# Low parts of the second gates ahead of phi's square sums in halves, and the first loop's rounding ahead of its normalising

## The chip, the cores and the metric

One core of a Trainium2 chip. The metric is the device time of the whole kernel in microseconds (us), here the median of 3 runs. Engines: PE (TensorE), DVE (VectorE), ACT (ScalarE), POOL (GpSimd), SP (queue of DMA issues).

## The reference, cut to what matters

One layer of a small language-model tower on 2 x 1024 tokens, width 192 (D), in float32:

```python
def _L0_tok_ref(input_ids, link_ids, wte, gamma, beta, W_proj, W_val, W_out, value_traces):
    tok = wte[input_ids]
    Q = _layer_norm(tok, gamma, beta) @ W_proj.T        # 8 heads of 64
    V = tok @ W_val.T
    Q_store, V_store = Q[:, :, :-2, :], V[:, :, 2:, :]  # Q_store masked by the link ids
    Q_erase = Q_store / norm(Q_store)
    erase = einsum('bhip,bhiq->hpq', Q_erase, einsum('bhip,hpq->bhiq', Q_erase, value_traces)) / denom
    traces = 0.99 * (value_traces - erase) + 0.1 * einsum('bhip,bhiq->hpq', Q_store, V_store) / denom
    return (shifted Q @ traces) @ W_out.T
def _L0_attn_ref(x, W_qkv, b_qkv, W_proj, b_proj, W_gp, alpha):
    gw = softmax(gelu(v @ W_gp))                        # 49 groups: the gates
    group_weight = gw @ gw.T
    attn = softmax(q @ k.T * scale * group_weight)
    out = ((1 - a) * attn + a * group_weight) @ v       # a = sigmoid(alpha)
    return out @ W_proj + b_proj
def _L0_ffn_ref(x, phi, ln_g, ln_b, w1, b1, w2, b2):
    phi_n = phi * rsqrt(sum(square(phi), axis=0) + 1e-6)   # sum over the 64 experts
    logits = einsum('bmd,npd->bmnp', x, phi_n)             # 64 experts x 16 slots
    D, C = softmax(logits, over tokens), softmax(logits, over slots)
    Xs = D.T @ x; hdn = gelu(layernorm(Xs) @ w1 + b1); Ys = hdn @ w2 + b2
    return C @ Ys
h = _L0_tok_ref(x, ...)
h = h + _L0_attn_ref(layernorm(h), ...)
h = h + _L0_ffn_ref(layernorm(h), ...)
```

## The kernel before, in words

Tokens are worked in 16 tiles (NT) of 128, 8 (KT) to a batch row. Float32 products are made of rounded parts: an operand is cast to a high part on ACT and DVE subtracts that from the original for the low part; `product` (L639) then sums five matmuls of high and low parts. Every engine has its own program, written out in order, and the programs meet only at semaphores: a wait stops all that stands behind it on its engine. So the order of the calls in each engine's loop over the steps `s` is what sets the order of the work.

**First loop (L745 on PE, L1306 on ACT, L1679 on DVE, L501 on POOL).** POOL gathers a tile's token rows (L483, an indirect DMA). DVE takes mean and variance (`stats`, L1613), POOL makes the power -0.5 and the factor of the mean (`front_factors`, L487), ACT normalises (`normalise`, L1237, xh), PE transposes (`tok_T`, L705), ACT rounds the transposed tile (`hi_parts`, L1252, XH), DVE makes the low part (`lo_parts`, L1638, XL), PE projects (`q_proj`, L722). ACT squares the projection and masks it (`squares`, `masked_q`, L1259, L1265), DVE sums the squares by head, and weights the queries (`norms`, `erase_q`, L1656, L1664, qw), PE adds up the Gram matrices (`grams`, L735). `masked` (L1248) and `cprime` (L713) feed the update of the traces. tok_T(i) needs lo_parts(i-2), q_proj(i) needs erase_q(i-3), normalise(i) needs the transposes of tile i-3. The row of beta (L1628) is the last row of the low weights; PE waited for it ahead of the first three products. DVE also copies that row to wpT (L1683) and scales the diagonal (L1686) in step 2, both needed only after the loop. SP issues the next weights when 11, 13, 14 and 15 tiles have their statistics (L419 to L427).

**Second loop (L1067 on PE, L1468 on ACT, L1914 on DVE, L588 on POOL).** Step s on PE: scores of tile s (`query_keys`), transposes of the exponentials of tile s-1 (`turn`, L940), group scores (L922), at odd steps a pair of u sums (`u_pair`), product with V of tile s-1 (`attend`), and in steps 2 and 3 the transposes of the second row's gates (`gw_T`). ACT rounds the transposed exponentials (et) and makes the scores' copy and the exponentials, and in steps 3 and 4 first rounds the gates (`gw_hi`, L1349). DVE, step by step: in steps 3 and 4 the gates' low parts first (`gw_lo`, L1774, gL), then etl (`turn`, L1855), the product of scores and gates (`z_tile`, L1844), `weight`, `finish` (L1868: the result of tile s-1 with its statistics), then `beside` (L1819), where the preparation of phi is spread over the steps: sum of the squares (L1823, after ACT's squares L1400), V's second low part (L1826), scaling in two halves (L1831), low parts (L1834, L1837). POOL makes the power of the sums. The transposes `turn(2)` and `turn(3)` on PE go to the banks that held the gates, and wait for gL (L947):

```python
                if i in (2, 3):
                    pe.wait_ge(m["gwT_taken"], GTS + i - 1)
```

In step 8 (FIRST_PASS - 1) PE transposes the first two tiles of x2, the input of the experts' logits; ACT rounds them (`x2_hi`, L1433) after normalising two more (`x2_tile`, L1423), DVE makes their low parts (`x2_lo`, L1879, X2L), and PE's turn(8) waits for these. From step 9 on two tiles of logits go into each step. They need phi's last low part (`ph_ready`).

After the second loop come the logits of the second row beside the dispatch, then 16 groups of 4 experts whose weights come in through a ring of four buffers, and the combination.

## Time and profile before

| what | us |
|---|---|
| median of 3 runs (lowest, highest) | 441.89 (441.79, 443.79) |
| the profiled execution | 441.72 |
| its span | 439.9 |
| busy in the span: PE, PE's weight loads | 416.6, 348.1 |
| DVE, ACT, POOL | 309.6, 233.6, 147.6 |
| share of the chain that ended last: PE, DMA, DVE, POOL, ACT | 73%, 11%, 6%, 4%, 3% |

The span is the time from the first to the last thing the profile shows; the run's own time is 1.8 us more. Busy time of an engine can lie beside that of another. The chain is followed back from the last instruction: at each step to what released it, or to the instruction before it on its engine. Starts are us from the span's start; the granted clock of PE is in parts of its full 2.4 GHz. Matmuls overlap their successors: the step from one start to the next is what one costs.

### The profile page before, as it was taken

How to read it: one execution, taken by the hardware profiler on the slowest of the kernel's cores; microseconds unless marked ns; L12 is line 12 of the kernel's file. 1: busy time of each engine (PE TensorE's matmuls, PEld its weight loads, DVE VectorE, ACT ScalarE, POOL GpSimd, SP SyncE). 2: the span in 40 equal slices, each digit the busy share in tenths (PEclk: the TensorE clock that was granted, in tenths of full speed). 3: DMA queues.
4: the chain of work that ended last, by engine and by line, in shares of the span. 5: the costliest groups of instructions: out<-in, count | busy, mean ns of one | idle time of the engine just before them, and what ended most of it. 6: DMA issues, size and time to landing. Idle time of an engine off the chain costs nothing.

```text
span 439.9 us, 8403 instructions
## 1 busy us (share of the span) xinstructions
PE 416.6 (95%) x3106; PEld 348.1 (79%) x3106; DVE 309.6 (70%) x776; ACT 233.6 (53%) x426; POOL 147.6 (34%) x243
## 2 busy tenths in 40 slices
PE   8899999999996899899999899999999799999995
PEld 6577766888896798788889888899956578778895
DVE  6799864877777788678988987777675335344464
ACT  5678735898443466644225758988854221212220
POOL 5885201773304732200002960023722222121310
PEclk9999999999998999999999999999999999999999
DMA  3126102001000000000000050009179999999305
GB/s 101 60 75 228 61 2 78 31 2 31 1 1 0 0 1 0 3 0 1 0 1 3 0 215 1 1 2 371 59 295 417 366 354 373 390 371 374 141 11 144
DMA packets 14232, 50.24 MB, mean 114 GB/s; under 512 B 3504, under 2 KB 8240, under 8 KB 9968
## 3 DMA queue, kind: packets, MB, share of 16 engines
q1 hardware_dynamic: 7584, 43.21, 26.1%
q0 software_dynamic: 2912, 3.96, 3.0%
q10 hardware_dynamic: 3696, 2.54, 1.9%
q8 instruction: 25, 0.41, 0.4%
q14 instruction: 15, 0.12, 0.1%
HBM read 46.53 MB, written 3.15 MB: 113 GB/s over the span
## 4 chain that ended last, share of the span: by engine, by line
PE 73%; DMA 11%; DVE 6%; POOL 4%; ACT 3%; issue 2%; SPq 0%; POOLq 0%; ACTq 0%; DVEq 0%
DMA w1r<-in_p_w 10%; PE ps L1035 8%; PE ps L1198 6%; PE ps L972 4%; PE ps L951 3%; PE ps L1139 3%; PE ps L976 3%; PE ps L1168 2%; PE ps L740 2%; PE ps L641 2%; PE ps L1015 2%; PE ps L1016 2%; PE ps L1017 2%; PE ps L1018 2%; PE ps L1019 2%
## 5 line engine op out<-in xcount | busy, mean ns | idle before, releaser
L1198 PE MATMUL ps<-ys,ct 128*128 128x192 f32 x256 | 45.2, 330 | 1.2 <-DMA ys<-ys_dram 1.2
L2038 DVE TENSOR_TENSOR res<-ps,res 128x384 f32<-128x384 f32 x64 | 35.7, 558 | 14.7 <-PE ps L1198 10.2
L1198 PEld LDWEIGHTS ps<-ys,ct 128*128 128x128 f32 x256 | 41.2, 190 | 4.6 <-issue 2.7
L520 POOL TENSOR_SCALAR ve<-mv 128x1 f32<-128x1 f32 x32 | 12.9, 402 | 89.6 <-DVE mv L1877 59.8
L629 POOL DMA_DIRECT2D ys<-ys_dram x32 | 19.6, 618 | 69.0 <-DMA ys_dram<-ysb 67.8
L1421 ACT CAST et<-ps 128x512 fp32r<-128x512 f32 x32 | 17.3, 590 | 41.5 <-PE ps L951 41.5
L1537 ACT ACTIVATE hs<-ps 128x384 f32<-128x384 f32 x16 | 7.9, 491 | 57.7 <-PE ps L1139 57.7
L2029 DVE COPY ysb<-ps 128x192 f32<-128x192 f32 x16 | 5.7, 357 | 38.8 <-PE ps L1168 38.8
L1413 ACT ACTIVATE zz<-zz,nmx 128x1024 f32<-128x1024 f32 x16 | 18.4, 1152 | 19.5 <-DVE nmx L1853 19.5
L1860 DVE TENSOR_TENSOR etl<-ps,et 128x512 fp32r<-128x512 f32 x32 | 20.7, 686 | 10.0 <-ACT et L1421 9.9
L1892 DVE CUSTOM_DVE_ANT_0 ec<-ps,zero 128x1024 f32<-128x1024 f32 x16 | 19.5, 1221 | 9.2 <-PE ps L1019 9.2
L1139 PE MATMUL ps<-w1r,xsT 128*32 128x384 f32 x256 | 24.0, 492 | 1.5 <-DMA w1r<-in_p_w 1.5
L972 PE MATMUL ps<-V,et 128*128 128x384 f32 x128 | 25.2, 339 | 0.0
L951 PE MATMUL ps<-ident,zz 128*128 128x128 f32 x128 | 17.6, 283 | 7.0 <-DVE gL L1778 4.5
L1543 ACT COPY ct<-ps 128x1024 f32<-128x1024 f32 x16 | 16.1, 1008 | 14.8 <-PE ps L1185 14.8
L951 PEld LDWEIGHTS ps<-ident,zz 128*128 128x128 f32 x128 | 15.2, 145 | 9.9 <-issue 7.5
L1850 DVE CUSTOM_DVE_ANT_0 zz<-scs,ps 128x1024 f32<-128x1024 f32 x16 | 19.5, 1221 | 4.7 <-PE ps L937 2.6
L972 PEld LDWEIGHTS ps<-V,et 128*128 128x128 f32 x128 | 22.2, 188 | 0.8 <-issue 0.2
L1035 PE MATMUL ps<-x2a,lsr 128*128 128x193 f32 x128 | 22.6, 327 | 0.0
L1035 PE MATMUL ps<-x2b,lsr 128*128 128x193 f32 x128 | 21.7, 327 | 0.7 <-ACT lsr L1452 0.7
L1035 PEld LDWEIGHTS ps<-x2b,lsr 128*128 128x128 f32 x128 | 20.9, 190 | 1.0 <-ACT lsr L1452 1.0
L1035 PEld LDWEIGHTS ps<-x2a,lsr 128*128 128x128 f32 x128 | 20.8, 190 | 0.2
(311 smaller groups left out, 1223.7 us busy)
## 6 DMA issues: line engine op xcount, KB each, us to landing
w1r<-in_p_w SPq DMA_DIRECT2D x16, 1152.0 KB, 19.1
w2r<-in_p_w SPq DMA_DIRECT2D x16, 1152.0 KB, 18.9
ys_dram<-ysb ACTq DMA_DIRECT2D x16, 96.0 KB, 8.8
ys<-ys_dram POOLq DMA_DIRECT2D x32, 48.0 KB, 7.2
phT<-in_p_phi SPq DMA_DIRECT2D x1, 1024.0 KB, 4.7
wT<-in_p_qkv SPq DMA_DIRECT2D x1, 774.0 KB, 4.4
out<-res SPq DMA_DIRECT2D x3, 192.0 KB, 3.4
out<-res ACTq DMA_DIRECT2D x3, 192.0 KB, 3.9
```

Of the source, the lines that this page charges most:

```text
L629: nc.gpsimd.dma_start(ys[rows, t % YR, b, :], y4[b]).then_inc(ys_loaded[t % YR], 16)
L951: last = nc.tensor.transpose(bank(4 + k // 4)[:, (k % 4) * P:(k % 4 + 1) * P], zz[:, i % 2, k * P:(k + 1) * P], ident[:])
L972: mm(d[:, 0:2 * D], et[:, c, :], V[b][:, c, :], start=(c == 0), stop=False, skip_group_check=True)
L1035: last = mm(d, ls(b, k)[:, t * P:(t + 1) * P], x2(i)[:, 0:1 + D], start=(k == 0 and t % 2 == 0), stop=(k == KT - 1), skip_group_check=True)
L1139: last = mm(bank(0)[32 * j:32 * j + 32, 0:HID], xsT[:, half, GE * g + j, :, :].rearrange("d b s -> d (b s)"), w1r[r][:, 3 * (j // 2) + j % ...
L1198: last = mm(bank(5 + q % 3)[:, h * D:(h + 1) * D], ct[:, u % 2, k + h, :], ys[:, t % YR, b, :], start=True, stop=True)
L1413: sc.activation(zz[:, i % 2, :], zz[:, i % 2, :], ACT.Exp, bias=nmx[:, i:i + 1], accum_out=rsum[:, i:i + 1]).then_inc(m["e_ready"], 1)
L1421: sc.copy(half_turned(et, half), bank(4 + half)).then_inc(m["et_copied_a"], 1)
L1850: v.tensor_tensor_reduce(zz[:, i % 2, :], scs[:], bank(2, 2), 1.0, LOWEST, ALU.mult, ALU.max, zmx[:, i:i + 1]).then_inc(m["z_ready"], 1)
L1860: v.tensor_tensor(half_turned(etl, half), bank(4 + half), f(half_turned(et, half)), ALU.subtract).then_inc(m["et_copied_v"], 1)
L1892: v.tensor_tensor_reduce(ec(i), bank(logit_bank(i), 2), bc(zero[:], [P, NS]), 1.0, LOWEST, ALU.add, ALU.max, mxC[:, i:i + 1]).then_inc(m[" ...
L2038: v.tensor_tensor(res[:, i:i + 2, :], bank(5 + q % 3)[:, 0:2 * D].rearrange("p (h d) -> p h d", h=2), res[:, i:i + 2, :], ALU.add).then_in ...
```

## The change

It moves work and splits one reduction; all sums and results are the same.

On PE the product of tile 0 waits for the beta row only ahead of its last matmul, and the products of tiles 1 and 2 no longer wait for it; the transposes of tile 3 go behind the product of tile 2, those of tile 4 behind grams(0). On ACT hi_parts(1) and (2) go one step earlier, ahead of normalise(2) and normalise(3), and squares and masked_q of tiles 0 and 1 ahead of normalise(3) and (4). On DVE lo_parts(0) goes ahead of the beta row, lo_parts(1) and the count ahead of stats(3); stats(4) goes between norms(0) and erase_q(0), stats(5) and (6) behind erase_q(1), stats(7) and (8) behind erase_q(2); the copy of the beta row and the diagonal go to steps 15 and 16. POOL makes the factors of tiles 3 and 4 ahead of the gathers of tokens 5 and 6.

In the second loop gw_lo(2) and (3) go from the start of steps 3 and 4 on DVE to the end of steps 2 and 3, ahead of `beside`; phi's squares are summed in two halves in steps 1 and 2 instead of at once in step 2; the rest of phi's preparation on DVE and ACT, and values_lo(1), go one step later; x2's first two tiles are rounded on ACT ahead of x2_tile(2) and (3), and x2_lo(0), (1) go ahead of `beside(8)` on DVE.

```diff
@@ -499,6 +499,8 @@
             front_factors(2)
...
             for i in range(3, NT):
+                if i < 5:
+                    front_factors(i)
                 if i + 2 < KT:
...
                 elif i == KT - 2:
@@ -511,7 +513,8 @@
                     gather(KT + 6)
...
                     gather(i + 4)
-                front_factors(i)
+                if i >= 5:
+                    front_factors(i)
             pool.wait_ge(m["xm_ready"], NT)
...
                 nc.gpsimd.memset(X1L[b][DB:P, 1, :].bitcast(F32), 1.0).then_inc(m["xl_ones"], 1)
@@ -558,7 +561,7 @@
             pool.wait_ge(m["pr_taken"], NT)
...
             values_hi(1)
-            pool.wait_ge(m["ph_summed"], 1)
+            pool.wait_ge(m["ph_summed"], 2)
             link(nc.gpsimd.tensor_scalar(prs[:], pss[:], 1e-6, None, ALU.add))
...
                                     mhalf[:, 0:2 * NP], ALU.pow).then_inc(m["ph_rsqrt"], 1)
@@ -636,12 +639,14 @@
             def filled(ins):
...
-            def product(dst, xH, xL, wAh, wAl, wB1, wB2):
+            def product(dst, xH, xL, wAh, wAl, wB1, wB2, last_row=False):
...
                 mm(dst, xH(1, P), wB1, start=False, stop=False)
+                if last_row:
+                    pe.wait_ge(m["beta_ready"], 1)
                 return mm(dst, xL(1, DB + 2), wB2, start=False, stop=True)
...
             def fill(name, free):
@@ -724,13 +729,11 @@
                 pe.wait_ge(m["xl_ready"], i + 1)
...
                     pe.wait_ge(m["qw_ready"], i - 2)
-                else:
-                    pe.wait_ge(m["beta_ready"], 1)
                 if i == 2:
...
                 product(q_bank(i), lambda h, n: XH[0:n, h, c], lambda h, n: XL[0:n, h, c],
-                        wpAh[:], wpAl[:], wpB1[:], wpB2[:]).then_inc(m["q_filled"], 1)
+                        wpAh[:], wpAl[:], wpB1[:], wpB2[:], last_row=(i == 0)).then_inc(m["q_filled"], 1)
...
                 pe.wait_ge(m["qw_ready"], i + 1)
@@ -745,7 +748,9 @@
             for s in range(1, NT + 5):
...
                     q_proj(s - 3)
-                if s < NT + 1:
+                if s == 5:
+                    tok_T(3)
+                elif s < NT + 1 and s != 4:
                     tok_T(s - 1)
...
                     keep_warm(4)
@@ -757,6 +762,8 @@
                     weigh(1)
...
                     grams(s - 5)
+                if s == 5:
+                    tok_T(4)
                 if s == NT + 2:
...
             pe.wait_ge(m["in_mix"], 16 * 5)
@@ -1304,15 +1311,18 @@
             act.wait_ge(m["mask_ready"], 1)
...
             for s in range(NT + 3):
-                if s == 1:
-                    hi_parts(0)
-                if 3 <= s < NT + 2:
+                if 1 <= s <= 3:
+                    hi_parts(s - 1)
+                if 5 <= s < NT + 2:
                     hi_parts(s - 2)
...
                     masked(s - 2)
+                if s in (3, 4):
+                    squares(s - 3)
+                    masked_q(s - 3)
                 if s < NT:
                     normalise(s)
-                if 3 <= s:
+                if 5 <= s:
                     squares(s - 3)
...
                 if s == NT:
@@ -1398,9 +1408,9 @@
...
                     sc.activation(phsq, phT[:], ACT.Square).then_inc(m["ph_squared"], 1)
-                if s in (5, 6):
-                    act.wait_ge(m["ph_scaled"], s - 4)
-                    sc.copy(phAh[:] if s == 5 else phB[:], phT[:, s - 5, :]).then_inc(m["ph_hi"], 1)
+                if s in (6, 7):
+                    act.wait_ge(m["ph_scaled"], s - 5)
+                    sc.copy(phAh[:] if s == 6 else phB[:], phT[:, s - 6, :]).then_inc(m["ph_hi"], 1)
...
                 act.wait_ge(m["s_filled"], i + 1)
@@ -1484,12 +1494,12 @@
                 if s == FIRST_PASS - 2:
...
                     x2_tile(1)
+                if s == FIRST_PASS - 1:
+                    x2_hi(0)
+                    x2_hi(1)
                 if FIRST_PASS - 1 <= s < FIRST_PASS + KT // PER_PASS - 2:
...
                     x2_tile(2 * (s - FIRST_PASS + 2) + 1)
-                if s == FIRST_PASS - 1:
-                    x2_hi(0)
-                    x2_hi(1)
                 for i in pass_tiles(s):
...
                         x2_hi(i + 2)
@@ -1616,25 +1626,6 @@
                 link(v.bn_aggr(mv[:, i, :], st6[:, i, :]))
...
-            stats(0)
-            dve.wait_ge(m["wp_hi"], 1)
-            remainder(wpAl[:], wpT[:, 0, :], gamA, wpAh[:])
-            stats(1)
-            dve.wait_ge(m["wp_hi"], 2)
-            remainder(wpB1[DB:P, :], wpT[DB:P, 1, :], gamB[DB:P], wpB1[DB:P, :])
-            stats(2)
-            dve.wait_ge(m["setup_hi"], 1)
-            beta_row = setup_bank("beta")[DB:DB + 1, :]
-            v.tensor_tensor(wpB2[DB:DB + 1, :], beta_row, f(wpB2[DB:DB + 1, :]), ALU.subtract).then_inc(m["beta_ready"], 1)
-
-            def count():
-
-                dve.wait_ge(m["cnt_filled"], 1)
-                link(v.tensor_scalar(cnt[:, 0:1], bank(6)[:, 0:1], float(HEADS), 1.0, ALU.mult, ALU.max))
-                link(v.reciprocal(cnt[:, 1:2], cnt[:, 0:1]))
-                v.tensor_scalar(cnt[:, 2:3], cnt[:, 1:2], -TRACE_DECAY * ERASE_LR, None, ALU.mult)
-                v.tensor_scalar(cnt[:, 3:4], cnt[:, 1:2], TRACE_LR, None, ALU.mult).then_inc(m["cnt_ready"], 1)
-
             def lo_parts(i):
...
                 lo = (b * SLOTS + 2 * k + 1) * Q
@@ -1644,6 +1635,27 @@
                 ins = v.tensor_tensor(XL[0:DB, 1, lo:lo + P], d[0:DB, P:2 * P], f(XH[0:DB, 1, lo:lo + P]), ALU.subtract)
...
+            stats(0)
+            dve.wait_ge(m["wp_hi"], 1)
+            remainder(wpAl[:], wpT[:, 0, :], gamA, wpAh[:])
+            stats(1)
+            dve.wait_ge(m["wp_hi"], 2)
+            remainder(wpB1[DB:P, :], wpT[DB:P, 1, :], gamB[DB:P], wpB1[DB:P, :])
+            stats(2)
+            dve.wait_ge(m["xl_ones"], 1)
+            lo_parts(0)
+            dve.wait_ge(m["setup_hi"], 1)
+            beta_row = setup_bank("beta")[DB:DB + 1, :]
+            v.tensor_tensor(wpB2[DB:DB + 1, :], beta_row, f(wpB2[DB:DB + 1, :]), ALU.subtract).then_inc(m["beta_ready"], 1)
+
+            def count():
+
+                dve.wait_ge(m["cnt_filled"], 1)
+                link(v.tensor_scalar(cnt[:, 0:1], bank(6)[:, 0:1], float(HEADS), 1.0, ALU.mult, ALU.max))
+                link(v.reciprocal(cnt[:, 1:2], cnt[:, 0:1]))
+                v.tensor_scalar(cnt[:, 2:3], cnt[:, 1:2], -TRACE_DECAY * ERASE_LR, None, ALU.mult)
+                v.tensor_scalar(cnt[:, 3:4], cnt[:, 1:2], TRACE_LR, None, ALU.mult).then_inc(m["cnt_ready"], 1)
+
             def wrap(b):
...
                 dve.wait_ge(m["xl_ready"], (b + 1) * KT)
@@ -1671,16 +1683,21 @@
...
-                if s <= 3:
-                    return {2: [3], 3: [4, 5]}.get(s, [])
+                if s < 4:
+                    return []
+                if s <= 6:
+                    return {4: [], 5: [5, 6], 6: [7, 8]}[s]
                 return [s + 2] if s + 2 < NT else []
-            dve.wait_ge(m["xl_ones"], 1)
-            for s in range(NT + 4):
-                if 2 <= s < NT + 2:
+            lo_parts(1)
+            count()
+            stats(3)
+            for s in range(4, NT + 4):
+                if s < NT + 2:
                     lo_parts(s - 2)
-                if s == 2:
+                if s == NT - 1:
                     v.tensor_copy(wpT[DB:DB + 1, 1, :], beta_row).then_inc(m["setup_taken"], 1)
+                if s == NT:
                     for r in range(2):
...
                         v.tensor_scalar(eyeP[rows, :], ident[rows, rows], TRACE_DECAY, None, ALU.mult)
@@ -1690,13 +1707,12 @@
                     v.tensor_scalar(cc[:, 0, :], bank(5)[:, 0:D], gamA, cnt[:, 3:4], ALU.mult, ALU.mult)
...
                                     ALU.mult, ALU.mult).then_inc(m["cc_ready"], 1)
-                if 4 <= s:
-                    norms(s - 4)
-                    erase_q(s - 4)
+                norms(s - 4)
+                if s == 4:
+                    stats(4)
+                erase_q(s - 4)
                 for i in ahead(s):
                     stats(i)
-                if s == 2:
-                    count()
                 if s == KT + 2:
...
@@ -1818,21 +1834,22 @@
...
-                if s == 2:
+                if s in (1, 2):
+                    h = s - 1
                     dve.wait_ge(m["ph_squared"], 1)
-                    v.tensor_reduce(pss[:], phsq.rearrange("d c (n p) -> d c p n", p=NP), AX, ALU.add
+                    v.tensor_reduce(pss[:, h, :], phsq[:, h, :].rearrange("d (n p) -> d p n", p=NP), AX, ALU.add
                                     ).then_inc(m["ph_summed"], 1)
-                if s == 3:
+                if s == 4:
                     values_lo(1)
-                if s in (4, 5):
+                if s in (5, 6):
                     dve.wait_ge(m["ph_rsqrt"], 1)
-                    h = s - 4
+                    h = s - 5
                     w = phT[:, h, :].rearrange("d (n p) -> d n p", p=NP)
                     v.tensor_tensor(w, w, bc(prs[:, h, :].unsqueeze(1), [P, NE, NP]), ALU.mult).then_inc(m["ph_scaled"], 1)
-                if s == 6:
+                if s == 7:
                     dve.wait_ge(m["ph_hi"], 1)
                     v.tensor_tensor(phAl[:], phT[:, 0, :], f(phAh[:]), ALU.subtract)
-                if s == 7:
+                if s == 8:
                     dve.wait_ge(m["ph_hi"], 2)
...
                 if s == FIRST_PASS + KT // PER_PASS:
@@ -1914,8 +1931,6 @@
...
             for s in range(NT + 1):
-                if 3 <= s < 3 + GTS:
-                    gw_lo(s - 1)
                 if 1 <= s <= NB:
...
                 if s >= 1:
@@ -1935,10 +1950,12 @@
                     u_add(s // 2)
...
                     finish(s - 1)
-                beside(s)
+                if 2 <= s < 2 + GTS:
+                    gw_lo(s)
                 if s == FIRST_PASS - 1:
...
                     x2_lo(1)
+                beside(s)
                 for i in pass_tiles(s):
```

## Rows read from the trace of the kernel before

**Rows 1.** The chain that ended last, in order of time (start us, us, what)
```profile
57.68 0.62 PE ps L740 x16
```

**Rows 2.** Timeline of PE, first loop (start us, us, engine line op out<-in [idle before <-releaser])
```profile
18.61 0.50 PE L641 MATMUL ps<-wpAh,XH 128*128 128x512 f32 x1 [0.74 <-DVE XL L1644]
...
21.47 0.50 PE L641 MATMUL ps<-wpAh,XH 128*128 128x512 f32 x1
...
22.75 0.27 PE L710 MATMUL ps<-ident,xh 128*128 128x128 f32 x1
```

**Rows 3.** Windows, one step of the first loop (stretch: us, busy us of each engine, clock, DMA)
```profile
27.18:30.04 2.86, 2.86 (x32) 2.21 (x28) 2.69 (x10) 2.28 (x5) 2.33 (x4) 1.00 0.17 50
```

**Rows 4.** Waits of PE over the span (for whom: us in total, times, longest)
```profile
PE ps L951 <- DVE gL L1778: 4.5, 2, 3.3
...
PE ps L951 <- DVE X2L L1887: 1.4, 1, 1.4
```

**Rows 5.** Timeline of DVE, second loop
```profile
128.60 0.42 DVE L1804 TENSOR_SCALAR uP<-ps,aw 128x192 fp32r<-128x192 f32 x1 [1.43 <-PE ps L892]
...
134.38 3.53 DVE L1823 TENSOR_REDUCE pss<-x2a 128x32 f32<-128x2048 f32 x1
...
146.18 1.73 DVE L1810 TENSOR_TENSOR V<-pr,V 128x1536 fp32r<-128x1536 f32 x1
147.82 0.68 DVE L1778 TENSOR_TENSOR gL<-ps,gD 128x512 fp32r<-128x512 f32 x1
...
182.50 0.29 DVE L1886 TENSOR_TENSOR X2L<-ps,X2H 128x128 fp32r<-128x128 f32 x1 [1.06 <-ACT X2H L1437]
```

**Rows 6.** Timeline of PE, second loop
```profile
138.66 1.94 PE L951 MATMUL ps<-ident,zz 128*128 128x128 f32 x8 [3.31 <-DVE gL L1778]
...
142.29 1.57 PE L972 MATMUL ps<-V,et 128*128 128x384 f32 x8
...
155.07 1.03 PE L951 MATMUL ps<-ident,zz 128*128 128x128 f32 x8
...
157.29 1.59 PE L972 MATMUL ps<-V,et 128*128 128x384 f32 x8
```

**Rows 7.** Timeline of ACT, second loop
```profile
133.81 0.57 ACT L1352 CAST gD<-ps 128x512 fp32r<-128x512 f32 x1
...
180.58 1.64 ACT L1428 ACTIVATE x2a<-res,nmr,rstd 128x192 f32<-128x192 f32 x4
```

**Rows 8.** Windows of the second loop (the clock stands ahead of the DMA share)
```profile
138.10:138.20 0.10, 0.00 (x0) 0.00 (x0) 0.10 (x1) 0.00 (x0) 0.10 (x1) 0.80 0.00 0
141.50:141.60 0.10, 0.10 (x1) 0.09 (x1) 0.10 (x1) 0.10 (x1) 0.10 (x1) 0.64 0.00 0
...
155.07:161.91 6.84, 6.84 (x43) 6.21 (x42) 5.80 (x14) 4.27 (x6) 1.74 (x4) 1.00 0.01 2
```

**Rows 9.** Timeline of ACT, first loop
```profile
16.12 0.60 ACT L1245 ACTIVATE xh<-tok,nmr,rstd 128x256 f32<-128x256 f32 x1 [2.19 <-POOL nmr L491]
...
17.67 0.37 ACT L1256 CAST XH<-ps 128x256 fp32r<-128x256 f32 x1
```

**Rows 10.** Timeline of GpSimd (POOL), first loop
```profile
22.87 0.58 POOL L490 TENSOR_TENSOR rstd<-ve,mhalf 128x1 f32<-128x1 f32 x1
23.56 0.26 POOL L491 TENSOR_SCALAR nmr<-mv,rstd 128x1 f32<-128x1 f32 x1
```

**Rows 11.** Timeline of DVE, first loop, one step from XL on
```profile
20.95 0.28 DVE L1643 TENSOR_TENSOR XL<-ps,XH 128x128 fp32r<-128x128 f32 x1
...
22.49 0.69 DVE L1668 TENSOR_TENSOR qw<-ps,fac 128x512 f32<-128x512 f32 x1
23.10 0.35 DVE L1615 BATCH_NORM_STATS2 st<-tok 128x6 f32<-128x192 f32 x1
```

**Rows 12.** Timeline of DVE, first loop, the copied beta row and the last XL
```profile
11.71 0.69 DVE L1683 COPY wpT<-ps 1x512 f32<-1x512 f32 x1
...
54.41 0.29 DVE L1643 TENSOR_TENSOR XL<-ps,XH 128x128 fp32r<-128x128 f32 x1 [0.95 <-ACT XH L1256]
```

More of the change, by code:

```diff
@@ L1617, in stats, with lo_parts @@
                 v.tensor_scalar(ve[:, i:i + 1], mv[:, i, 1:2], 1e-5, None, ALU.add).then_inc(m["front_stats"], 1)
+            def lo_parts(i):
+                b, k = divmod(i, KT)
+                lo = (b * SLOTS + 2 * k + 1) * Q
+                dve.wait_ge(m["xh_copied"], i + 1)
+                d = bank(i % 2)
+                v.tensor_tensor(XL[:, 0, lo:lo + P], d[:, 0:P], f(XH[:, 0, lo:lo + P]), ALU.subtract)
+                ins = v.tensor_tensor(XL[0:DB, 1, lo:lo + P], d[0:DB, P:2 * P], f(XH[0:DB, 1, lo:lo + P]), ALU.subtract)
+                ins.then_inc(m["xl_ready"], 1)
             stats(0)
@@ L1636, in count @@
                 v.tensor_scalar(cnt[:, 3:4], cnt[:, 1:2], TRACE_LR, None, ALU.mult).then_inc(m["cnt_ready"], 1)
-            def lo_parts(i):
-                b, k = divmod(i, KT)
-                lo = (b * SLOTS + 2 * k + 1) * Q
-                dve.wait_ge(m["xh_copied"], i + 1)
-                d = bank(i % 2)
-                v.tensor_tensor(XL[:, 0, lo:lo + P], d[:, 0:P], f(XH[:, 0, lo:lo + P]), ALU.subtract)
-                ins = v.tensor_tensor(XL[0:DB, 1, lo:lo + P], d[0:DB, P:2 * P], f(XH[0:DB, 1, lo:lo + P]), ALU.subtract)
-                ins.then_inc(m["xl_ready"], 1)
             def wrap(b):
```

## The prediction

> **What bounds the kernel now.** The page first: by its busy time TensorE (PE) is the engine that sets the span. The chain of waits, in order of time, then says where it is something else than PE's own work. In the first loop the chain runs over PE alone up to the last group of traces' products at 57.68 us [rows 1], from the product of tile 2 at 18.61 on, which stood 0.74 us for DVE's low part [rows 2]: a step of the loop is 2.86 us of PE, and VectorE (DVE) is busy 2.69 us of each [rows 3], so nearly full too. The waits between engines name what PE stood still for in the second loop: the low parts of the gates (gL) twice, 4.5 us in all, and the first low parts of x2 (X2L) once, 1.4 us [rows 4]. The rest of the second loop, the dispatch and the experts follow PE, or transfers that are issued when a step of the experts ends; nothing there has a start of its own, so I let a shift at the end of the second loop reach the end whole.
>
> **The second loop, part by part.**
> (1) Low parts of gates 2. Now DVE adds up the squares of phi in one 3.53 us reduction from 134.38 to 137.91 and only then, at the start of step 3, makes gL [rows 5]. PE's transposes of step 3 wait for that: 3.31 us [rows 6]. In the change gL stands ahead of the reduction. Its input, ScalarE's (ACT) cast, is done at 133.81+0.57 = 134.38 [rows 7], just when DVE has finished tile 1. So gL runs 134.45 to 135.13. PE's stop began at 138.66-3.31 = 135.35, and then it no longer stops: 3.3 to 3.4 us gained, I take 3.4.
> (2) The clock. Behind that stop the granted clock is at its lower level, 1.2 GHz, from about 138.16 to 141.57; the fall came 2.8 us after PE stopped [rows 8]. From the transposes to the first matmul with V it took 142.29-138.66 = 3.63 us; the same work at 2.4 GHz takes 157.29-155.07 = 2.22 us [rows 6]. Without the stop there is no reason for the fall: 1.41 us gained.
> (3) The reduction in halves. Each half has 1024 of 2048 elements per partition, about 3.53/2 = 1.77 us. Half 0 goes behind tile 0, where DVE was free for 1.43 us ahead of 128.60 [rows 5]; it ends at about 128.9 and makes u_take(1) 0.3 us late, whose result PE wants only when it comes to V, behind transposes and scores. Half 1, behind gL, ends at 136.8, some 0.15 us after the next etl could start; the product behind etl waits for ACT's copy of the scores in any case. GpSimd starts its power 1 us earlier than before. Cost 0; without the covers 0.45.
> (4) Low parts of gates 3. They were at 147.82, behind values_lo(1) of 1.73 us [rows 5], which moves to step 4. Finish(2) ends about 6.75 us after the transposes of its step, gL takes 0.68, so PE may go on 7.45 after them, and PE itself needs 6.84 for such a step [rows 8] and 0.4 for four gate transposes (a good third of the 1.03 that eight take, with their tail [rows 6]): 7.2. Of the wait of 4.5-3.3 = 1.2 us [rows 4] 0.25 to 0.3 stays: 0.9 gained. values_lo(1) in step 4 ends about where the next etl starts (7.8 us into the step): 0.
> (5) phi's scaling and rounding go one step later, each into DVE and ACT time of the same kind; the last low part moves behind x2_lo, is over by the end of step 8 and is needed in step 9: 0. If it came late, its 1.2 us would be what PE waits for.
> (6) In step 8 ACT rounds x2's first two tiles ahead of the next two normalisings, 1.64 us for four instructions [rows 7]. DVE's X2L started at 182.50 after standing 1.06 for that [rows 5]; now it starts when finish(7) is done, 181.44. PE waited 1.4 us for it [rows 4]: 1.06 gained, I take 1.1; 0.3 to 0.4 stays.
> Sum of the second loop: 3.4+1.4+0.9+1.1 = 6.8 us.
>
> **The first loop.** Here the change first gains and then, by my working, loses more.
> (7) XL(0) goes ahead of the beta row and the last row of the first product waits for that instead: about 0.4 us earlier at the first product. XH(1), XH(2) go ahead of the normalising of tiles 2 and 3, which in before stood waiting 2.19 us for GpSimd's factors [rows 9]. So XL(1) and XL(2) come about 2.5 and 4 us earlier; the third product starts at about 16.1 instead of 18.61 and the fourth (tile 3), with tile 4's transposes done, at 19.3 instead of 21.47 [rows 2]. 2.1 to 2.2 us ahead at this point.
> (8) But the statistics of tiles 4 and 5 move back on DVE: 4 behind norms(0), 5 and 6 behind erase_q(1). Follow them. Squares of tile 0 are there at 15.1; norms(0) to 16.2, stats(4) to 16.9; GpSimd's power and factor (0.58+0.26, with gaps 1.0 [rows 10]) to 17.9; xh(4) 0.60 to 18.5; XH(3) 0.37 [rows 9] to 18.8. XL(3) starts at 18.85. From XL to the weighted queries DVE takes 22.49-20.95 = 1.54, these 23.10-22.49 = 0.61, one tile's statistics 0.64 (0.75 until they can be used) [rows 11], so stats(5) starts at 21.0 and ends at 21.75. Factors until 22.8, xh(5) until 23.4, and PE transposes tile 5 at 23.5: before, it did so at 22.75 [rows 2]. PE is through with the fourth product at 20.5: it stands for about 2.9 us, and the lead of 2.1 is a lag of 0.75.
> (9) It grows. ACT's in-order queue holds squares(2), masked_q(2) and XH(4) behind xh(5): 23.4+0.5+0.6+0.4 = 24.8, XL(4) to 25.3, PE's product of tile 4 there instead of 21.47+2.86 = 24.3, 1.0 late. DVE's step 6 carries two tiles' statistics: XL(5) comes 1.54+0.61+1.28 = 3.4 us after XL(4), at about 28.3, that of tile 5 at 28.9 instead of 27.2: 1.7 late. From here PE needs 2.86 a step and has no idle time to catch up with [rows 3]. I take 1.8 us lost, carried to the end.
> (10) The copy of the beta row (0.69) and the diagonal, which is shorter, go to steps 15 and 16, where DVE has no statistics to make and waits 0.95 us for ACT before the last XL [rows 12]: 0; without that cover 0.1 to 0.4. SP's loads wait for the counts 11 to 15 of the statistics, 1.8 us later, and are used from 62 us on: 0. Gathers 5 and 6 go behind factors 3 and 4 and are still ahead of stats(5).
>
> **Sum.** -6.8+1.8 = -5.0. The profiled execution took 441.72 us with a span of 439.9, the median of the runs shown is 441.89; so 441.7-5.0 = **436.7 us**, 1.1% less.
>
> **A rule against it.** A stop of 3.31 us was followed by the lower clock; stops of 1.2 and 1.4 were not. The new one of about 2.9 lies between, just past the 2.8 after which the fall came [rows 8]. Priced by rows: 1.41 us of delay at most [rows 6], of which the waits that DVE forces on PE right after (0.3+0.5+0.3 us in my working of steps 6 to 8) take up some: 0.4 to 1.4, say 1.0. The Trainium skill, page "TensorE: Matmul & The Clock Gate", section "What's actually happening", says that the watch on the engine's activity runs by itself and isn't set by the kernel, so that the same stop can meet it differently; by that rule the fall is a matter of phase, and the time would be 437.7. No row here shows a stop of this length.
>
> **Rivals and chances.**
> A, as above, clock stays up: 436.7; 0.45.
> B, the clock falls in the first loop's new stop: 437.7; 0.25. It also adds a stretch at 1.2 GHz near 23 us.
> C, the first loop keeps its lead: if the factors of tile 5 come early enough (a queue orders itself otherwise than I read it), 2.1 gained instead of 1.8 lost: 436.7-3.9 = 432.8. For it: PE had 0.74 us [rows 2] and one more stop like it to give there, and the lead of 2.1 us is real up to tile 3. Against it: the place of stats(5) in the code. 0.12.
> D, the change doesn't do what it says: gL(2) still waits, for ACT's cast, because ACT comes late with it, and the half sums fall into DVE's way: only (4) and (6) with a half of (1) and (2) are gained, 4.4, less 1.8: 439.1; 0.08.
> E, no gain in all (the transfers of the experts' weights set the end from a start of their own): 441.7; 0.05. Against it: they are issued at the end of a step that PE sets.
> F, slower: PE's waits in steps 6 to 8 keep the clock at 1.2 GHz over several stretches of 3.4 us. Each stretch costs 1.41 us [rows 6, 8]; from the fourth on the whole gain is used up (5.0-4x1.41 = -0.6), and with six it is 445.2. What decides is whether PE's standing still comes back after step 8; by (9) it doesn't. 0.05.
>
> Range: A and B with the bounds of (1) to (4) and (6) (5.7 to 7.3) and of the first loop's loss (1.2 to 3.2) give 435.6 to 439.2; taking in part of C and D: 433.6 to 439.8. About 0.5% (2.2 us) is what a measurement of this kernel tells from no change. Faster by more: A, B, C, most of D: 0.88. Within: the rest of D, E: 0.08. Slower: 0.04.
>
> **What would show it.** Right: no wait of PE for gL(2), under 0.5 us for gL(3), 0.4 for X2L; clock 1.00 throughout the second loop; that loop 6.8 us shorter. In the first loop product 3 about 2 us earlier, then PE idle near 20.6 for 2.9 us with ACT's xh as releaser, and the end of the loop (57.68) 1.8 later. Wrong: a first loop that ends earlier than 57.7, or a wait of over 1 us for gL or X2L.

## The result, and the profile after

Six runs of the changed kernel have a median of 438.41 us (437.75 to 439.04), six of the kernel before 442.54 us: ratio 0.9904 with a 95% interval of [0.9887, 0.992], 0.96% less time. The forecast was 436.7 us with a range of 433.6 to 439.8, so faster, as forecast. The medians are 4.1 us apart, where 5.0 were forecast. The two profiled executions are 2.9 us apart: 438.86 us with a span of 437.0 us and a mean granted clock of 0.991, against 441.72, 439.9 and 0.995. The working below is that of the profiles.

The page after (span; busy time of each engine; the granted clock in 40 slices):
```profile
span 437.0 us, 8402 instructions
...
PE 417.7 (96%) x3106; PEld 349.2 (80%) x3106; DVE 309.9 (71%) x777; ACT 233.6 (53%) x426; POOL 147.8 (34%) x243
...
PEclk9969999999999999999999999999999999999999
```
The waits of PE after (for whom: us in total, times, longest):
```profile
PE ps L715 <- ACT xh L1252: 4.1, 3, 2.9
...
PE ps L958 <- DVE X2L L1904: 0.2, 1, 0.2
```
Against [rows 4] the wait for gL is gone and that for X2L is 0.2 us. A wait for ACT's xh has come, 2.9 us long, and the one low digit of the clock stands in the third slice (each has 10.9 us), right behind it.

The timeline of PE, second loop, after:
```profile
132.10 1.04 PE L958 MATMUL ps<-ident,zz 128*128 128x128 f32 x8
...
138.95 1.06 PE L958 MATMUL ps<-ident,zz 128*128 128x128 f32 x8
...
141.20 1.59 PE L979 MATMUL ps<-V,et 128*128 128x384 f32 x8
...
146.43 1.06 PE L958 MATMUL ps<-ident,zz 128*128 128x128 f32 x8
...
180.14 1.06 PE L958 MATMUL ps<-ident,zz 128*128 128x128 f32 x8 [0.20 <-DVE X2L L1904]
```
The transposes of steps 2, 3 and 4 (the first, second and fourth row) follow each other without a stop for another engine, after 6.85 and 7.48 us; from the transposes at 138.95 to the matmul with V it is 2.25 us instead of 3.63 [rows 6]. DVE's rows of the same stretch:
```profile
130.79 1.86 DVE L1840 TENSOR_REDUCE pss<-x2a 128x16 f32<-128x1024 f32 x1
...
138.11 0.69 DVE L1794 TENSOR_TENSOR gL<-ps,gD 128x512 fp32r<-128x512 f32 x1
138.72 1.91 DVE L1840 TENSOR_REDUCE pss<-x2a 128x16 f32<-128x1024 f32 x1
...
152.45 1.95 DVE L1826 TENSOR_TENSOR V<-pr,V 128x1536 fp32r<-128x1536 f32 x1
```
The low parts of gates 2 now stand ahead of the second half sum. (All times here are 3.7 us later than in the forecast's working, since the first loop ends later.)

The timeline of PE, first loop, after:
```profile
15.84 0.53 PE L644 MATMUL ps<-wpAh,XH 128*128 128x512 f32 x1
...
19.35 0.50 PE L644 MATMUL ps<-wpAh,XH 128*128 128x512 f32 x1 [0.20 <-DVE XL L1635]
...
23.65 0.48 PE L715 MATMUL ps<-ident,xh 128*128 128x128 f32 x1 [2.87 <-ACT xh L1252]
...
26.61 0.80 PE L644 MATMUL ps<-wpAh,XH 128*128 128x512 f32 x1
...
30.97 0.50 PE L644 MATMUL ps<-wpAh,XH 128*128 128x512 f32 x1
...
61.94 1.13 PE L682 MATMUL ps<-wpT,cc 128*128 128x512 f32 x2
```
And the windows around the stop (stretch: us, busy us of PE, PEld, DVE, ACT, POOL, clock, DMA share, GB/s):
```profile
22.50:23.00 0.50, 0.00 (x0) 0.00 (x0) 0.13 (x1) 0.00 (x1) 0.36 (x2) 1.00 0.00 0
23.00:23.20 0.20, 0.00 (x0) 0.00 (x0) 0.00 (x0) 0.20 (x1) 0.08 (x1) 0.67 0.00 0
24.00:26.00 2.00, 2.00 (x14) 1.37 (x14) 1.05 (x3) 1.27 (x4) 1.67 (x3) 0.50 0.22 66
...
29.80:30.00 0.20, 0.20 (x3) 0.14 (x2) 0.17 (x2) 0.19 (x1) 0.20 (x1) 0.76 0.00 0
```
The product of tile 2 starts 2.77 us earlier than before, that of tile 3 2.12 us earlier [rows 2]. Then PE stands 2.87 us for xh(5). During the stop the clock falls to 1.2 GHz, and it stays there to 29.9 us: since the clock is either 1.00 or 0.50, the mean of 0.67 puts the fall at 23.07 and that of 0.76 the return at 29.90, 6.83 us together. Matmuls of 512 columns come 0.42 us apart instead of 0.23.

What released PE can be followed back in the chain of waits after (start us, us, what):
```profile
20.60 0.69 DVE qw L1680
...
21.29 0.28 DVE st L1625
...
21.81 0.16 DVE ve L1627
22.05 0.56 POOL rstd L490
22.70 0.27 POOL nmr L491
23.00 0.61 ACT xh L1252
23.65 0.48 PE ps L715
```
That is step (8) of the forecast row by row: statistics of tile 5 behind the weighted queries, then GpSimd, ACT, PE.

Three rows of the kernel before, for comparison, the product of tile 5, the end of the first loop and the transposes of step 8:
```profile
27.19 0.50 PE L641 MATMUL ps<-wpAh,XH 128*128 128x512 f32 x1
...
58.23 1.13 PE L677 MATMUL ps<-wpT,cc 128*128 128x512 f32 x2
...
183.52 1.06 PE L951 MATMUL ps<-ident,zz 128*128 128x128 f32 x8 [1.36 <-DVE X2L L1887]
```
**Where the time went.** The last product of the first loop (the matmuls of wpT and cc) starts at 61.94 instead of 58.23: 3.71 us lost. From there to the transposes of step 8 it is 118.20 us instead of 125.29: 7.09 us gained. The rest of the gap of 2.9 us is the stretch of the experts, first to last gelu: 87.05 instead of 86.59 us. That one was 86.7 to 87.7 us long in the profiles below, and 89.0 in one, so before's was at its short end.

### The profile page after: what moved, and what is told of

Its sections match the earlier page's. It is cut to its first block, busy times and chain, and to the rows that moved or that the text cites. A ratio compares the mean times of both kernels' runs of the same rounds, so it can differ in the third digit from the quotient of the medians.

```text
span 437.0 us, 8402 instructions
## 1 busy us (share of the span) xinstructions
PE 417.7 (96%) x3106; PEld 349.2 (80%) x3106; DVE 309.9 (71%) x777; ACT 233.6 (53%) x426; POOL 147.8 (34%) x243
## 4 chain that ended last, share of the span: by engine, by line
PE 75%; DMA 12%; DVE 4%; POOL 3%; ACT 2%; issue 2%; SPq 0%; POOLq 0%; ACTq 0%; DVEq 0%
DMA w1r<-in_p_w 11%; PE ps L1042 8%; PE ps L1205 6%; PE ps L979 5%; PE ps L1146 3%; PE ps L958 3%; PE ps L983 3%; PE ps L1175 2%; PE ps L743 2%; PE ps L644 2%; PE ps L1022 2%; PE ps L1023 2%; PE ps L1024 2%; PE ps L1025 2%; PE ps L1026 2%; PE ps L922 2%
## 5 line engine op out<-in xcount | busy, mean ns | idle before, releaser
L523 POOL TENSOR_SCALAR ve<-mv 128x1 f32<-128x1 f32 x32 | 11.9, 372 | 83.2 <-DVE mv L1894 53.4
L583 POOL TENSOR_TENSOR xve<-xve,mhalf 128x2 f32<-128x2 f32 x8 | 7.4, 921 | 40.0 <-DVE xve L1984 40.0
L483 POOL DMA_INDIRECT tok<-in_p_wte,ints x18 | 18.3, 1018 | 6.1 <-issue 3.4
```

What stands on the lines that cost most here:

```text
L483: nc.gpsimd.indirect_dma_start(tok[:, g, :], None, a["p_wte"], bass.IndirectOffsetOnAxis(ap=ints[:, g:g + 1], axis=0)).then_inc(gathered[g ...
```

## The experiments

Theory: the second loop gives 7 us by itself; of the first loop's 3.7 us about half is the order of the statistics, and half the lower clock behind the new stop. Rival: the first loop's loss is order alone and the clock is hidden behind DVE's waits, or the two loops' effects don't add up. In the short diffs "-" is the changed kernel's code where nothing else is said; they are cut, and the first two name the hunks by one line each.

**The two halves of the change.** The first run keeps only the edits of the second loop, the second only those of the first.
```diff
 # e1: the first loop's hunks taken back
-            lo_parts(0)       # ahead of the beta row, hi_parts(0..2) early
+            stats(0); stats(1); stats(2)   # before's order
 # e2: the second loop's hunks taken back
-                if 2 <= s < 2 + GTS: gw_lo(s)
+                if 3 <= s < 3 + GTS: gw_lo(s - 1)   # ahead of u_take
```


> Only the edits of the second loop; the first loop is that of before. Theory (the two loops' effects add up, the second loop gains what its own stops and low clock cost): first loop ends at 57.7 as before, no low clock in it, second loop 7.1 us shorter, 6.6 to 7.1 us less than before in all, that is 3.6 less than the changed kernel. Rival (part of what the second loop gained came from its later start, or a shorter lead at its end is lost in the experts' transfers): 3 to 5 us less than before.

> Only the edits of the first loop. Theory (order of the statistics 1.8 us, low clock behind the stop of 2.9 us another 1.9): 3.0 to 3.7 us slower than before, first loop's end at 61.4. Rival (order alone, the low clock is hidden under DVE's own lateness): 1.8 slower, end at 59.5.

Measured (the ratio is to runs of the kernel before on the same chip, the clock that of the profile): 435.15 us (ratio 0.9837 [0.9811, 0.9863], clock 0.999) and 445.79 us (1.0062 [1.0038, 1.0085], clock 0.986). The second loop's edits gain 1.6% alone and shorten that loop by 7.06 us (118.23 us); the first loop's edits alone make the kernel slower. In the second run PE's first loop (first line) and second loop:
```profile
23.68 0.47 PE L715 MATMUL ps<-ident,xh 128*128 128x128 f32 x1 [2.88 <-ACT xh L1252]
...
141.97 1.94 PE L958 MATMUL ps<-ident,zz 128*128 128x128 f32 x8 [3.29 <-DVE gL L1794]
```
and its windows:
```profile
22.00:22.20 0.20, 0.00 (x0) 0.00 (x0) 0.20 (x1) 0.00 (x0) 0.13 (x1) 0.85 0.00 0
22.20:22.40 0.20, 0.00 (x0) 0.00 (x0) 0.17 (x2) 0.00 (x0) 0.20 (x1) 0.50 0.00 0
...
28.80:29.20 0.40, 0.40 (x4) 0.27 (x3) 0.40 (x2) 0.26 (x1) 0.24 (x2) 0.79 0.09 31
```
The low clock lasted from 22.14 to 28.97 us, again 6.83 us, though the fall came 1.3 us after PE stopped and not 2.3. The loop ended at 61.50. The halves add up: 7.06 and -3.27 us here, 7.09 and -3.71 in the changed kernel. The 0.44 us between the two first loops, whose code is the same, go with the phase of the fall. An earlier fall meant an earlier return, so PE had work for 5.29 us of the low stretch (23.68 to 28.97) and not for 6.25 (23.65 to 29.90), and the product of tile 5 started at 30.53 and not at 30.97. The second loop of this run had its old stop back, and behind it 3.4 us at the lower clock.

**Order and clock apart.** The changed kernel with matmuls of ones by ones, whose result nobody reads, in the place of the stop:
```diff
             for s in range(1, NT + 5):
                 if 3 <= s < NT + 3:
                     q_proj(s - 3)
+                if s == 6:
+                    for _ in range(18):    # e12: range(12)
+                        mm(bank(1)[:, 256:384], ones[:], ones[:], start=True, stop=True)
```


> The changed kernel with 18 matmuls of ones that nobody reads, put on PE between the product of tile 3 and the transposes of tile 5, into the stop of 2.9 us; the rest is the same. Theory: the clock stays up, the transposes of tile 5 come at the same 23.6, the first loop ends at 59.5 instead of 61.4: 1.9 us less than the changed kernel. Rival (PE's low clock costs nothing since DVE is late anyway): same time as the changed kernel, end at 61.4 with a clock of 1.00.

> As the filler of 18, which took 4.0 us and ran 1.0 us past the stop, but with 12 matmuls, 2.6 us by the same rate, so that it ends inside the stop. Theory (order of the statistics 1.7 to 1.8 us, low clock the rest of 3.7): transposes of tile 5 at 23.7 as in the changed kernel, product 5 at 28.9, the last stretch of the first loop at 59.9 to 60.0 against 61.94 there and 58.2 before; 1.9 to 2.0 us less than the changed kernel. Rival (DVE would be late by 1 us less anyway, or the clock's part is what the longer filler already showed): 60.2 as with 18.

Measured: 437.55 us (0.9908 [0.9874, 0.9942], clock 0.998) and 437.43 us (0.9893 [0.9862, 0.9924], clock 0.998). In neither profile did the clock fall there; both means are below 1 only by the last 2 us of the span. 18 of them filled 4.0 us (36 passes), longer than the stop, so a shorter one was run; its PE rows:
```profile
20.68 2.84 PE L753 MATMUL ps<-ones 128*128 128x128 f32 x24
23.71 0.33 PE L715 MATMUL ps<-ident,xh 128*128 128x128 f32 x1 [0.19 <-ACT xh L1255]
...
25.55 0.50 PE L644 MATMUL ps<-wpAh,XH 128*128 128x512 f32 x1
...
29.04 0.51 PE L644 MATMUL ps<-wpAh,XH 128*128 128x512 f32 x1 [0.21 <-DVE XL L1638]
...
60.15 1.12 PE L682 MATMUL ps<-wpT,cc 128*128 128x512 f32 x2
```
PE waits for the same xh(5), but now by filler, and the transposes are at 23.71. The loop ends at 60.15, and at 60.19 with the longer filler, which so cost nothing more: its surplus went into waits that PE has there without it. So the order costs 60.15-58.23 = 1.92 us and the clock 61.94-60.15 = 1.79 us, in these profiles; with the first loop's edits alone (end at 61.50) the clock's part would be 0.44 less. The clock's part is built up in the two next products: 26.61-25.55 = 1.06 late at tile 4, 30.97-29.04 = 1.93 at tile 5. The whole time does not show the filler's gain: 0.86 and 0.98 us between medians taken on different chips, ratios of 0.9908 and 0.9893 against 0.9904 with intervals that overlap. In the other ten runs of the two fillers the mean clock was 0.991 to 0.994 five times, so in some of them it must have been low for longer than in the profiles; where, no profile shows. The split rests on the place of single rows.

**The place of the statistics.** First, only the list that hands them out one step earlier; then the statistics of tile 4 ahead of norms(0), of tile 5 behind it, and GpSimd's factors and gathers in before's order:
```diff
-                    return {4: [], 5: [5, 6], 6: [7, 8]}[s]
+                    return {4: [5], 5: [6, 7], 6: [8]}[s]      # e4
+                    return {4: [6], 5: [7], 6: [8]}[s]         # e8
...
+                if s == 4: stats(4)                            # e8
                 norms(s - 4)
-                if s == 4: stats(4)
+                if s == 4: stats(5)                            # e8
                 erase_q(s - 4)
```


> The changed kernel with the statistics of tile 5 one step earlier (behind erase_q(0), where DVE stood for 1.33 us), 6 and 7 in the next, 8 in the one after. Theory (place of stats(5) in DVE's order makes the stop): the stop of 2.87 falls to about 1.5, no low clock, first loop ends at 58.2 (0.5 later than before): 3.2 us less than the changed kernel. Rival (the stop comes from GpSimd's gathers 6 and 7 ahead of the factors of tile 5): stop stays at over 2.5.

> The changed kernel with the statistics early again: tile 4 ahead of norms(0), tile 5 between norms(0) and erase_q(0), one tile a step from there, and GpSimd's gathers in the order of before. Theory (the earlier rounding is good, the later statistics are what cost): no stop over 0.8 us in the first loop, clock up, first loop ends 0 to 0.4 us earlier than before (57.3 to 57.7): 3.7 to 4.1 us less than the changed kernel, and as fast as or faster than the second loop's edits alone. Rival (DVE, nearly full, gives the lead back in any order): 0.5 us or more behind the second loop's edits alone.

Measured: 436.13 us (0.9853 [0.9827, 0.9879]) and 434.6 us (0.9828 [0.9811, 0.9845], 434.16 to 434.71). With the list alone, PE's rows are:
```profile
22.09 0.33 PE L715 MATMUL ps<-ident,xh 128*128 128x128 f32 x1 [1.20 <-ACT xh L1252]
...
58.51 1.12 PE L682 MATMUL ps<-wpT,cc 128*128 128x512 f32 x2
```
The stop shrinks to 1.20 us, the clock stays up, and the loop ends only 0.28 us later than before: 3.4 of the 3.7 us are back from moving the statistics of tiles 5 and 7, some 0.75 us of DVE's time each, one step ahead. With the statistics of tile 4 earlier too, and GpSimd's order back:
```profile
18.89 0.69 PE L740 MATMUL ps<-qm,qw 128*64 128x64 f32 x16 [0.66 <-DVE qw L1677]
...
20.25 0.50 PE L641 MATMUL ps<-wpAh,XH 128*128 128x512 f32 x1 [0.31 <-DVE XL L1632]
...
57.48 1.12 PE L679 MATMUL ps<-wpT,cc 128*128 128x512 f32 x2
```
From the transposes at 9.77 to the end of the loop no stop is over 0.66 us, and the end is 0.75 us ahead of before's. So the loop kept some of the early rounding's lead here, but not 2.1 us; the same kernel once more, below, kept less.

Is that better than the second loop's edits alone? Both again, on one chip:

> The second loop's edits alone once more, on one chip with the next. Theory: 1.6% less than before, its first loop's last stretch starts at 58.1.

> The changed kernel with early statistics once more, beside the second loop's edits alone. Theory (its first loop ends 0.6 us earlier, 57.5 against 58.1): 0.3 to 0.9 us less than those. Rival (the transfers of the experts' weights take the lead back): no difference beyond 0.3.

Measured: 435.5 us (435.02 to 436.3) and 434.93 us (434.34 to 435.47), loop ends 58.19 and 57.99. 0.57 us between medians (0.13%) with ranges that overlap: not settled. The loop's lead over before was 0.24 us this time and not 0.75: DVE waited 1.02 us for the gathered rows of a tile, until 22.84, before it could take the next statistics, and PE then 1.01 us for XL, until 24.04. So earlier statistics run into the arrival of the rows, which differs from run to run. Both kernels beat the one before by 1.6 to 1.8%, and by these ratios the changed one by 0.7 to 0.9%.

**The second loop's parts.** Each takes one part back in the kernel with the second loop's edits alone ("-" is that kernel):
```diff
 # e5: low parts of the gates ahead of u_take, one step later
-                if 2 <= s < 2 + GTS: gw_lo(s)
+                if 3 <= s < 3 + GTS: gw_lo(s - 1)
 # e6: the whole sum in step 2, GpSimd waits for one
-                if s in (1, 2): h = s - 1; v.tensor_reduce(pss[:, h, :], ...)
+                if s == 2: v.tensor_reduce(pss[:], ...)
 # e7: x2_hi(0), x2_hi(1) behind the next two x2_tile
```


> Second loop's edits alone, but the gates' low parts go back to the start of steps 3 and 4 (the half sums stay in steps 1 and 2). Theory: gL(2) waits for the second half sum only, PE stands for about 1.8 us in step 3 instead of 3.31 and the clock does not fall (stops of 1.2 and 1.4 were not followed by it); in step 4 no or a small stop: 1.8 to 2.3 us more than the second loop's edits in full. Rival (the move of gL is all, halving does nothing without it): the clock falls again, 4.5 or more.

> Second loop's edits alone, but phi's squares are summed at once in step 2, behind gL. Theory: no stop for gL(2), but etl(2) on DVE comes 1.6 to 1.7 us later, at 138.6 instead of 136.9, PE waits 0.8 us for it ahead of the low products with V, the product of scores and gates and so the exponentials and gL(3) come later too: 1 to 2.5 us more than with halves. Rival (slack in the step takes it up): within 0.3 us.

> Second loop's edits alone, but ACT rounds x2's first tiles behind the two normalisings again. Theory: the stop of PE ahead of turn(8) is back at 1.2 to 1.4, 1.1 us more than with the order changed. Rival (DVE's order alone made the gain): within 0.3 us.

Measured: 437.75, 437.32 and 436.78 us (ratios 0.9905 [0.9883, 0.9926], 0.9887 [0.9866, 0.9909], 0.9879 [0.9857, 0.9901]). By the medians that is 2.6, 2.2 and 1.6 us more than with none of them taken back, but on another chip and with the experts' stretch in it; in the profiles the first gelu starts 1.72, 1.51 and 1.18 us later (315.90 with none taken back). PE's rows, gates back:
```profile
136.92 1.06 PE L951 MATMUL ps<-ident,zz 128*128 128x128 f32 x8 [1.59 <-DVE gL L1778]
```
whole sum:
```profile
139.35 1.29 PE L976 MATMUL ps<-V,etl 128*128 128x192 f32 x8 [0.31 <-DVE etl L1860]
...
144.44 1.06 PE L951 MATMUL ps<-ident,zz 128*128 128x128 f32 x8 [1.06 <-DVE gL L1778]
```
x2 back:
```profile
177.62 1.06 PE L951 MATMUL ps<-ident,zz 128*128 128x128 f32 x8 [1.36 <-DVE X2L L1888]
```
With the sum in halves but the gates late, PE stops 1.59 us and the clock stays up. The halving alone, with the later place of the rest of phi's preparation, so takes off 1.7 of the 3.31 us and with it the fall of the clock. With the gates early but the sum whole, the 3.7 us block no longer stops PE at step 3; it makes etl 0.31 us late and, a step on, gL(3) 1.06. So each of the two edits alone takes only a part of the 3.31+1.19 us of both gL stops, and leaves 1.4 to 1.6; to have all of it, both are needed.

**The clock's price in the second loop.** The kernel before, with matmuls in the place of its own stop:
```diff
+                if i == 2:
+                    pe.wait_ge(m["z_ready"], 3)
+                    for _ in range(24):
+                        mm(bank(2)[:, 0:P], ident[:], ident[:], start=True, stop=True)
                 if i in (2, 3):
                     pe.wait_ge(m["gwT_taken"], GTS + i - 1)
```


> The kernel before with 24 matmuls of the identity, which nobody reads, put on PE into its stop ahead of turn(2) in the second loop; the wait for gL stays. It measures the clock's part by itself. Theory: turn(2) comes at the same 138.7, the clock stays at 2.4 GHz, from turn(2) to the first matmul with V it takes 2.2 us instead of 3.63: 1.4 us less than before. Rival (the work behind the stop is held by DVE and ACT, not by the clock): same time as before within 0.4 us.

Measured: 445.06 us (1.005 [1.0027, 1.0072]), slower than the kernel before, and in part by my sizing: each of the 24 took two passes, 0.22 us, so that they filled 5.4 us and held the transposes to 140.55, 1.89 late. What it was for is still there:
```profile
140.55 1.04 PE L955 MATMUL ps<-ident,zz 128*128 128x128 f32 x8
...
142.78 1.57 PE L976 MATMUL ps<-V,et 128*128 128x384 f32 x8
...
149.96 1.06 PE L955 MATMUL ps<-ident,zz 128*128 128x128 f32 x8 [2.00 <-DVE gL L1782]
```
The clock stayed at 1.00 in this loop, and the work from the transposes to V took 2.23 us, not 3.63: 1.40 us, the term of step (2). As a whole time it proves nothing: at the transposes of step 8 this profile is 1.31 us behind before's, but at the end 3.7. In the experts' stretch, 2.4 us longer than before's, PE had waited 1.64 and 2.10 us for transfers, up to 347.86 and 352.43, and the granted clock was at its lower level from 353.3 to 356.7. How much of the 2.4 us that took was not measured.

## Why the prediction was right, and where it was off

The sign and the range came as forecast, and so did the course of both loops but for one low stretch of the clock. In the profiles, which the forecast was worked out from, the gain is 2.9 us instead of 5.0: 0.3 more in the second loop, 1.9 less in the first, 0.46 less in the experts' stretch. That the median of 438.41 lies only 1.7 us off is in part luck: six runs of the kernel before have a median of 442.54, 0.8 us above the 441.7 that the forecast started from.

**(1) and (2), right.** No wait for gL(2); the step from the transposes of step 2 to those of step 3 is 6.85 us instead of 10.26, so 3.41 (forecast 3.4), and the clock gives 1.40 by the filler (1.41).
**(3), right in effect.** A half takes 1.86 to 1.91 us and not 1.77, with no wait of PE behind it. That the halving costs nothing was right; that with the gates' low parts early it is still worth 1.5 us, as its undoing shows, I had not priced.
**(4), a little low, and its reason off.** The step is 7.48 us, 7.45 forecast, but no stop of PE stands in it: PE's own work fills it, for which I had reckoned 7.2. Steps (2) and (4) together gave 9.99-7.48 = 2.51 us for 2.3.
**(5), right.** The next steps show no new wait of PE.
**(6), right.** 0.20 us of wait stays (0.3 to 0.4 forecast); taking the part back costs 1.18 us for 1.1.
Sum of the second loop 7.09 us for 6.8.

**(7), right.** Tile 3 at 19.35, forecast 19.3. **(8), right.** Stop of 2.87 us (2.9) for xh(5), transposes at 23.65 (23.5). **(9), right at the clock it assumed.** With the clock held up by the filler, the product of tile 4 is at 25.55 (25.3), of tile 5 at 29.04 (28.9), and the end 1.92 us late (1.8). **(10), right:** no wait of PE there.

**The rivals C to F** did not come. C fell with step (8), D and E with the second loop's 7.09 us, which reached the end but for 0.46 us, F because the waits of steps 6 to 8 ended with that stretch.

**The step that failed is the clock in the first loop's stop**, which the sum put at 0 and my rival B at 1.0. The end of the loop came 3.71 us late and not 1.8. The pricing of that clock went wrong in three ways. Its chance: I put A ahead, 0.45 against 0.25, because the stop lay just past the 2.8 us after which the fall came. But both profiles that have this stop show the low stretch. The mean clocks of the other runs point the same way, no more: 6.83 us low are 0.8% of the mean clock, and the six runs of the changed kernel had 0.991 to 0.992 four times and 0.994 and 0.995 once each. The ten with the second loop's edits alone had 0.997 to 1.0 nine times and 0.994 once; a mean doesn't say where the clock was low. Its length: I took the 3.4 us stretch of the second loop for it; here it is 6.83 us, twice. And its price: I took 1.41 us as the most it can be, a bound that holds only for that length. From the transposes of tile 5 to the product of tile 5 PE took 27.19-22.75 = 4.44 us before and 30.97-23.65 = 7.32 in the changed kernel: 2.88 more. With the clock held up it took 29.04-23.71 = 5.33, so 0.89 of the 2.88 would have been lost to waits all the same (1.1 in my working), and 1.79 are left at the end of the loop. The price goes by the part of the low stretch in which PE works: 1.41 us for the 2.91 us from 138.66 to 141.57 [rows 6, 8], 2.88 for 6.25, and 30.53-23.68-4.44 = 2.41 for 5.29 with the first loop's edits alone. That is 0.46 to 0.48 us per us in all three.
With 1.8 in place of 0 the forecast's sum is 436.7+1.8 = 438.5 us; the profiled execution took 438.86.

The Trainium skill, page "TensorE: Matmul & The Clock Gate", section "What's actually happening", was read as leaving the fall to the phase of a watch that runs by itself. That the fall came 2.3 us after PE stopped in one profile and 1.3 us in the other, at the same stop, agrees. That the stop was spared altogether in some execution no profile here shows.

Open: why the low clock lasted 6.83 us here and 3.41 in the second loop. The windows show PE full in both once it works again, and no run varied what might differ. The experts' stretch of 86.6 to 87.7 us is left unexplained too, and so is what there set off the low stretch of the one profile with 89.0; it moves the total by about a us, and by 2.4 in that one.

## What to carry to other kernels

A lead that an early operation gains in a loop is worth what the latest input of the next tiles lets through: here 2.1 us were gone, and 1.9 more with them, because statistics of 0.75 us a tile had slid behind other work on DVE. Where an edit makes a new stop of the matmul engine of some 3 us, price it twice, once as idle time and once as the lower clock, the latter by how long the engine would work at it, less the waits that it would have had anyway. And when a change has a part that gains and one that loses, run the parts alone: the second loop's edits gave 1.6%, the whole change 1.0%, and with one list of statistics handed out a step earlier the whole gave 1.5%.

## What the runs showed of the hardware

- One stretch of low clock can last 6.83 us (first loop, both profiles) and another 3.41 us (second loop) after stops of 2.87 and 3.31 us. In the two loops, stops of 2.00 us and less were followed by none. In the experts' stretch one of 2.29 us was followed by none in one profile (18 fillers), and a pair of 1.64 and 2.10 us was followed by 3.4 us of low clock in another (24 fillers).
- A low stretch cost 0.46 to 0.48 us for each us of it in which PE worked (1.41 in 2.91, 2.88 in 6.25, 2.41 in 5.29).
- Matmuls nobody reads, put in the place of a stop, kept the clock at 1.00 there in the profiles of all three kernels that had them.
- A plain 128x128 float32 matmul runs as two passes and takes 0.22 us, twice what I had sized for.
- The same DVE instructions took longer in some places: the addition into V 1.73 us [rows 5], but 1.95 in the changed kernel and 2.02 with the 24 fillers; the whole sum 3.53 us before and 3.72 behind gL. What works beside them there was not varied, so no cause is shown.
